# Values of two pairs of heads in one product of 512 columns, two blocks of tokens per period; a ring of seven weight tiles, three buffers of values

## The reference, cut to what matters

```python
x = x + attn(cond(x, fside, fside, w, u, cond_512))
x = x + ffn(cond2(x, ...))          # silu(x W1') * (x W3'), fwht, W2'

def attn(y):                        # y as (2, 1024, 512): 16 heads of 128
    q, k, v = y @ Wq, y @ Wk, y @ Wv            # each to 16 heads x 128
    for seg in 8 segments of 128 tokens:        # mem, z carried on
        att_dot = softmax(causal(q k' / sqrt(128))) @ v
        att_mem = (elu(q)+1) @ mem / ((elu(q)+1) @ z)
        delta   = v - (elu(k)+1) @ mem / ((elu(k)+1) @ z)
        mem, z  = mem + (elu(k)+1)' @ delta, z + sum(elu(k)+1)
        out     = (beta * att_mem + (1-beta) * att_dot) @ Wo
```

## Time and profile before

| | before |
|---|---|
| median of 3 runs | 1582.96 us (1582.52 to 1583.41) |
| profiled execution | span 1581.4 us; its own time is that span and 1.6 us around it, 1583.0 us |
| PE busy | 1547.0 us (98%), 9574 matmuls |
| DVE, ACT, POOL busy | 77%, 49%, 39% |
| a period without Wo | about 26.3 us |
| a burst period | about 48.7 us |
| period 0 starts, period 31 starts | 60.1 us, 1038.7 us |

### The profile page before, as it was taken

One profiled execution on the slowest core, in us unless ns is written; L12 is line 12 of the kernel. 1 busy time (PEld: TensorE's weight loads), 2 busy tenths in 40 slices (PEclk: granted clock), 3 DMA queues, 4 the chain that ended last, 5 costly groups with the idle time before them and its releaser, 6 DMA issues.

```text
span 1581.4 us, 26868 instructions
## 1 busy us (share of the span) xinstructions
PE 1547.0 (98%) x9574; PEld 1377.9 (87%) x9574; DVE 1219.7 (77%) x2719; ACT 782.1 (49%) x1687; POOL 615.2 (39%) x433
## 2 busy tenths in 40 slices
PE   4899999999999999999999999999999999999999
PEld 2699989999999999998999999989888888888887
DVE  8889888787878888778775773665897888687785
ACT  3576566445535626535546552653554443344442
POOL 3666585322222222222001000134664465666662
PEclk9999999999999999999999999999999999999999
DMA  5375685595473485474467547348211222311111
GB/s 177 124 246 191 223 292 195 180 392 184 161 276 127 154 286 201 147 254 160 174 228 280 210 171 283 110 141 279 88 54 54 60 89 72 107 46 62 54 41 54
DMA packets 109381, 262.04 MB, mean 166 GB/s; under 512 B 11200, under 2 KB 36160, under 8 KB 107840
## 3 DMA queue, kind: packets, MB, share of 16 engines
q1 hardware_dynamic: 90384, 227.28, 40.5%
q10 hardware_dynamic: 18864, 33.04, 6.5%
HBM read 212.03 MB, written 48.25 MB: 165 GB/s over the span
## 4 chain that ended last, share of the span: by engine, by line
PE 90%; DVE 6%; issue 2%; DMA 1%; ACT 1%; POOL 0%; SPq 0%; ACTq 0%; DVEq 0%
PE psG L595 17%; PE psG L597 17%; PE psG L596 17%; PE psX L771 4%; PE psX L726 3%; PE psX L595 3%; PE psX L597 3%; PE psX L596 3%; PE psZ L752 3%; PE psZ L743 3%; PE psZ L751 2%; PE psZ L597 2%; PE psY L597 2%; PE psY L596 2%; PE psZ L596 2%
## 5 line engine op out<-in xcount | busy, mean ns | idle before, releaser
L2076 POOL TENSOR_TENSOR wl<-stage,wh 128x512 fp32r<-128x512 f32 x160 | 233.5, 1481 | 147.4 <-ACT wh L1597 144.7
L595 PE MATMUL psG<-yh,wh 128*128 128x512 f32 x646 | 263.1, 407 | 0.0
L597 PE MATMUL psG<-yh,wl 128*128 128x512 f32 x646 | 253.0, 392 | 0.0
L596 PE MATMUL psG<-yl,wh 128*128 128x512 f32 x646 | 252.1, 390 | 0.0
L2144 POOL TENSOR_TENSOR vs<-v,omb 128x512 f32<-128x512 f32 x64 | 92.1, 1460 | 388.9 <-PE psX L726 216.0
L597 PEld LDWEIGHTS psG<-yh,wl 128*128 128x128 f32 x646 | 121.3, 188 | 26.8
L595 PE MATMUL psG<-wh,yh 128*128 128x256 f32 x480 | 141.6, 295 | 0.0
L595 PEld LDWEIGHTS psG<-yh,wh 128*128 128x128 f32 x646 | 121.9, 189 | 20.9 <-DVE sg L1274 0.3
L596 PEld LDWEIGHTS psG<-yl,wh 128*128 128x128 f32 x646 | 121.9, 189 | 20.5
L597 PE MATMUL psG<-wh,yl 128*128 128x256 f32 x480 | 135.7, 283 | 0.0
L596 PE MATMUL psG<-wl,yh 128*128 128x256 f32 x480 | 135.7, 283 | 0.0
(11 more groups left out here) (279 smaller groups left out, 4291.6 us busy)
## 6 DMA issues: line engine op xcount, KB each, us to landing
wh<-high_o SPq DMA_DIRECT2D x52, 512.0 KB, 3.6
wl<-low_o SPq DMA_DIRECT2D x52, 512.0 KB, 4.7
stage<-in_w SPq DMA_DIRECT2D x64, 256.0 KB, 3.1
wh<-high_k SPq DMA_DIRECT2D x23, 512.0 KB, 3.7
wl<-low_k SPq DMA_DIRECT2D x23, 512.0 KB, 5.0
wh<-high_q SPq DMA_DIRECT2D x23, 512.0 KB, 4.1
wl<-low_q SPq DMA_DIRECT2D x23, 512.0 KB, 5.8
wh<-high_v SPq DMA_DIRECT2D x22, 512.0 KB, 4.0
```

Source lines behind the costliest of these rows:

```text
L595: e.matmul(out, lh, rh, start=first, stop=False, skip_group_check=check)
L596: e.matmul(out, lh, rl, start=False, stop=False, skip_group_check=check)
L597: return e.matmul(out, ll, rh, start=False, stop=last, skip_group_check=check)
L2076: e.tensor_tensor(lo, raw, hi, ALU.subtract).then_inc(p_wl, 1)
```

## The change

- **Values.** `v_block` takes the place of `v_part`: one call makes values of two pairs of heads (`couple(n)` and the next) for 128 tokens. The moving operand has 512 columns: 256 from each of two tiles of the ring, through one view of the array `parts` (`parts[:, p, x:y+1:y-x, ...]`). Periods 2m and 2m+1 each make two of the four blocks of 128 tokens (`tokens_of`). The calls of a part of 12 matmuls of 256 columns become parts of 6 of 512. Periods 0 and 30 are `bare`: period 0 makes its values at its end, period 30 makes none.
- **Ring.** `wh` and `wl` become one array `parts` with 7 tiles (`NRING`). A tile of values is held over two periods (`held`), except after a burst, where the second period fetches it again as kind "w". The stream grows from 204 to 218 tiles.
- **Buffers.** The two buffers of values become one array of six halves; `HALVES` says which two a period reads.
- **Order of the stream.** k, q before v in period 0; v, v, (o...), k, q in even periods; k, q in odd ones (w, w first after a burst); k, v, v, q in period 6 (`SWAPPED`), where values also stand behind the keys on PE. The places up to which ACT, POOL and SP go follow from `ENDS`.
- **Others.** The scan tiles (1, 0, 1..3) come after (0, 2, 0..3); some semaphores are merged; `dynamic_dma_scratch_size=1024`.

```diff
-NRING = 6
+NRING = 7
...
+def couple(n):
+    return n + 2 - n % 2
+def tokens_of(n, half):
+    return 2 * (n % 2) + half
+def value_kind(n):
+    return "w" if n % 2 and is_burst(n - 1) else "v"
 def weight_stream():
...
+        a = couple(n)
+        values = [(value_kind(n), a), (value_kind(n), a + 1)]
+        has = a < NN and (n % 2 == 0 or is_burst(n - 1))
+        keys = [("k", n + 1), ("q", n + 1)]
+        if n == 0:
+            stream += keys + values
+        elif n == SWAPPED:
+            stream += keys[:1] + values + keys[1:]
+        else:
+            if has:
+                stream += values
+            if is_burst(n):
+                stream += [("o", 8 * (n // 4 - 1) + i) for i in range(8)]
+            stream += keys
...
-            def v_part(n, half, part):
-                b, i = n // NG, PLACE["v", n]
+            def v_block(n, half, part):
+                i, k = value_tiles(n)
                 if part == 0:
                     wait_split(w, i)
-                    wait_y(b)
-                    w.wait_ge(a_qm, 2 * (n - 1) + half + 1)
-                rows = slice(256 * half + 128 * part, 256 * half + 128 * part + 128)
-                for c in range(NC):
-                    cols = slice(256 * c, 256 * c + 256)
-                    m = three(G[half][:, 256 * part:256 * part + 256], yh[b % 2][:, c, rows], yl[b % 2][:, c, rows],
-                              hi[:, cols], lo[:, cols], c == 0, c == NC - 1)
+                    wait_split(w, k)
+                    wait_y(couple(n) // NG)
...
+                rows = slice(128 * tokens_of(n, half), 128 * tokens_of(n, half) + 128)
+                x, y = SLOT[i], SLOT[k]
+                for c in (0, 1) if part == 0 else (2, 3):
+                    hi, lo = (parts[:, p, x:y + 1:y - x, 256 * c:256 * c + 256] for p in range(2))
+                    m = three(G[half][:, :], yh[b % 2][:, c, rows], yl[b % 2][:, c, rows], hi, lo, c == 0, c == NC - 1)
...
-                split_hi(here + 3)
+                split_hi(o + 2 if burst else end - 1 if more else end)     # ACT, between exp_s(n, 0) and exp_s(n, 1)
...
-                keep(here + 2)
-                load_w(here + (6 if burst and n > 4 else 4))
+                keep(o + 1 if burst else end - 2)
+                load_w((o + 5 if n > 4 else o + 3) if burst else end + 1)
```

More of the change, by code:

```diff
@@ L189, with value_tiles, value_halves, blocks_by @@
 SLOT, BEFORE = places()
+def value_tiles(n):
+    return sorted((PLACE[value_kind(n), couple(n) + p] for p in range(2)), key=SLOT.__getitem__)
+def value_halves():
+    at = {0: (0, 1), 1: (2, 3)}
+    for a in range(2, NN, 2):
+        one = sorted(at[a - 3] if a > 2 else (4, 5))
+        two = sorted(at[a - 2])
+        at[a], at[a + 1] = (one[0], two[0]), (one[1], two[1])
+    return at
+HALVES = value_halves()
+def blocks_by(n, half):
+    return 2 * n + half + 1
+def values_of(n):
+    return 0 if n < 2 else blocks_by(n // 2 * 2 - 1, 1)
+def pick(t, x, y):
+    return t[:, x:y + 1:y - x] if x < y else t[:, x:y - 1 if y else None:y - x]
 def first_of(kind, m):
@@ L269, in adaln_attn_ffn @@
         yl = [sb(ctx, f"yl{i}", [P, NC, T], F32R) for i in range(2)]
[L270 to L271 removed]
+        parts = sb(ctx, "parts", [P, 2, NRING, 1024], F32R)
         stage = [sb(ctx, f"stage{i}", [P, 512]) for i in range(NSTAGE)]
@@ L321, in adaln_attn_ffn @@
         sk = sb(one, "sk", [P, 2, T])
-        v = [sb(one, f"v{i}", [P, NSEG, 2, VW]) for i in range(2)]
+        v = sb(one, "v", [P, 6, 2, 2, VW])
         vs = sb(one, "vs", [P, NSEG, 2, P])
@@ L898, in tensor @@
                     kq_part(nx, "q", 1, 1)
+                if n == 0:
+                    for half in range(2):
+                        v_block(n, half, 0)
+                        v_block(n, half, 1)
             w.wait_ge(v_f1, 2)
@@ L1913, in scalar @@
                 if burst:
-                    copy_v(nx, 1)
-                split_hi(here + 4)
+                    copy_v(n, 1)
+                split_hi(o + 3 if burst else end if more else end + 1)
                 behind(n, 3)
-                if more and n > 0 and not burst:
-                    copy_v(nx, 1)
+                if n == SWAPPED:
+                    copy_kq(nx, "k", 1, G[1])
+                    exp_kq(nx, "k", 1, G[1])
+                elif more and not bare and not burst:
+                    copy_v(n, 1)
                 if burst:
-                    split_hi(here + 6)
+                    split_hi(o + 5)
                 copy_pt(n)
@@ L1946, in scalar @@
                 if more:
-                    split_hi(here + (12 if burst else 6))
+                    split_hi(end + (1 if burst else 2))
                     copy_kq(nx, "q", 0, G[0])
                     exp_kq(nx, "q", 0, G[0])
-                    split_hi(here + (14 if burst else 6))
+                    split_hi(end + (3 if burst else 2))
                     copy_kq(nx, "q", 1, G[1])
+                    if n == 0:
+                        exp_kq(nx, "q", 1, G[1])
                 else:
@@ L2190, in gpsimd @@
                 more = nx < NN
-                here = PLACE["v", nx] if more else PLACE["1", 0]
+                end, o = ENDS[n], ENDS[n] - 10
                 if n >= LATE_V:
@@ L2194, in gpsimd @@
                 behind(n, 0)
-                split_w(here + 3)
+                split_w(o + 2 if burst else end - 1 if more else end)
                 behind(n, 1)
@@ L2200, in gpsimd @@
                     euv(4)
-                split_w(here + 4)
+                split_w(o + 3 if burst else end if more else end + 1)
                 behind(n, 3)
                 if burst:
-                    split_w(here + 6)
+                    split_w(o + 5)
                 behind(n, 4)
-                split_w(here + (9 if burst else 5))
+                split_w(o + 8 if burst else end + 1 if more else end + 2)
                 behind(n, 5)
@@ L2210, in gpsimd @@
                 if burst:
-                    split_w(here + 11)
+                    split_w(end)
                 if n == 4:
@@ L2215, in gpsimd @@
                 if burst:
-                    split_w(here + 13)
+                    split_w(end + 2)
                 if more:
-                    split_w(here + (14 if burst else 6))
+                    split_w(end + (3 if burst else 2))
                 else:
```

234 lines of the change are left out of this document (142 added, 92 removed).

## The result

The changed kernel takes 1610.73 us (median of 5 runs, 1607.71 to 1613.79) against 1582.96: a ratio of 1.0175, interval [1.0164, 1.0187]. It is slower by 27.8 us; 13.8 were forecast, and 1605 was the end of the range. The direction and four of the five periods with new waits were right; two sizes were not, and one wait was not in the sum. The profiled execution spans 1608.4 us, 27.0 more than before.

What follows compares the result with a forecast made beforehand. PE was taken as the bound, busy 1547.0 of 1581.4 us. Terms -6.0 + 9.0 + 1.5 + 4 + 3 + 2.3 = +13.8 on 1583.0 gave 1596.8, said as 1597; range 1584 to 1605.

Steps and rivals of the forecast that it cites:

- A: Matmuls of values in 30 periods: 120 parts, each 0.05 us shorter with 512 columns, 6.0 us less.
- the small gap cost: Rival: a matmul's own cost is small, wide values matmuls save some 2 us in all, 1601 us; chance 0.05.
- the two pieces: Rival: a moving operand in two pieces costs 65 us over 720 matmuls, 1648 us; chance 0.02.
- B: Period 0: later load of values 2, split between ACT's exponentials, makes PE wait for the second one: +9.0 us.
- C: Behind period 0's wait: PE's matmuls run at the lower clock for a while, +1.5 us.
- D: Period 4: the copy of P on ACT stands behind one more split tile, 19 instead of 18, +4 us.
- the signs: What would show it: PE's waits in periods 0, 4 (on pT or a Wo tile) and 6, low clock, shorter period 30.
- E: Period 6: values wait for y's low part, behind POOL's split of queries 7, +3 us.
- F: Period 30: values no longer fill between the memory's steps, so PE waits, +2.3 us.
- the fifth: Rival: waits in periods 4 and 6 pass on to the o tiles behind them, above 1606 us; chance 0.05.

Runs made afterwards that it cites:

- wide_alone: Kernel before, only the values' matmuls reshaped to 6 of 512 columns per part, orders and ring kept, values not the reference's: 1578.23 us, ratio 0.9969.
- experiment 1: Changed kernel with period 0's old order: values 2 loaded before queries 1 are kept, and split behind both exponentials: 1600.31 us.
- experiments 2 and 3: Changed kernel with one half of period 0's old order each, only the earlier load of values 2, or only its later split: 1604.47 and 1607.0 us.
- experiment 5: Changed kernel with tile o0 split on ACT and POOL at the end of period 3 instead of between period 4's exponentials: 1606.55 us.
- Experiment 6: Changed kernel with ACT's split of keys 6 moved behind the copy of the last queries, into period 5: 1607.35 us.
- y_first: Changed kernel with POOL's split of queries 7 in period 6 put behind the low part of y: 1606.22 us.
- p0_split_only: Changed kernel with values 2 split behind both exponentials of period 0, but still loaded only after keeping queries 1: 1607.0 us.
- q_copy_first: The same run as Experiment 6: changed kernel, last queries copied ahead of the split of keys 6: 1607.35 us.
- four_orders: Changed kernel with four order edits together: period 0's old order, y first in period 6, o0 split early, last queries copied first: 1587.20 us.
- y_slack: Changed kernel with all order edits: four_orders plus moved period 30 keys, scan steps, POOL's scaling, period 6 values and period 4 EUV: 1581.06 us.
- p0_order: The same run as experiment 1: changed kernel with period 0's old load and split order: 1600.31 us.

## Why the prediction was wrong

- **A (-6.0)** was right in kind and near in size. In the table 4.7 us are read in periods 1 to 3 and 7 to 29, and some 0.6 more stand within periods 4 to 6; wide_alone, where nothing else changes, gives 4.9 (3.0 to 6.8). Of the rivals the small gap cost and the two pieces are out.
- **B and C (+9.0, +1.5)** were right in place and mechanism: the wait grew by 9.8. Period 0 without 5.9 us for its values grew by 11.2; experiment 1 takes out 12.0, of which 2.2 are more than the wait, so C's 1.5 was a little low. That load and place are both needed was argued from one row; experiments 2 and 3 show that each leaves a wait of its own, on the next split. (The fixed cost that stands behind B from the Trainium skill, DMA: Bandwidth & Descriptors, section Anatomy of one DMA, is given there for DMAs that GpSimd issues; these loads are issued by SyncE, and the sum did not use it.)
- **D (+4)** measured 5.9, and its working does not hold. The count is wrong: up to o4 the stream has 17 tiles before the change, not 18, and 19 after it, so the copy of P stands behind two tiles more. By the working's own 4.7 us a tile that would be 8.5. Nor does that pace set the lateness. The tiles lay landed in their stage buffers until their place on ACT came: values 6 from about 151 to 169.21 and values 7 from about 159 to 175.16 (the rows below), o0 from 176 to 185.67, some 9 us, and the next load went out only behind such a split (o0's at 171.36). I had this order and did not price it. PE met the lateness at Wo's tiles, which the signs had named beside P. Only o0's place was tested (experiment 5); that of values 6 and 7 was not.
- **Period 5 (+4.0)** had no term. With E it is the step that failed most: "where a split stands ahead of something that PE needs" was asked of period 0 only. The same question at the end of period 4 gives keys 6 ahead of the copy of qT. Experiment 6 takes out all of it.
- **E (+3)** measured 8.0. The working gave 4.3 to 5.2 us of wait; I then cut it to 3 for short waits that it would replace, with no row for them, and charged no clock. Measured: 6.5 of wait, for POOL's rows were longer (5.6 for 4.2), and about 2 of clock, as y_first shows.
- **F (+2.3)** came out: 2.1 us of waits in two rows, period 30 shorter by 3.5. There was luck in it: with the same waits the period takes 1.5 us more in half of the traces (last section).

```profile
169.21 1.14 ACT L1695 ACTIVATE parts<-stage 128x512 fp32r<-128x512 f32 x2
...
175.16 1.14 ACT L1695 ACTIVATE parts<-stage 128x512 fp32r<-128x512 f32 x2
```

Together: D 1.9, period 5 4.0, E 5.0, B and C 0.7, the start 0.7, and A 1.3 short in its rows less 0.5 that the end gave make 13.1 of the 13.2 us between +13.8 and the span's +27.0. The rival that came nearest was the fifth, at a chance of 0.05. Its way (D passed on) was not the true one: separate places were.

## What to carry to other kernels

When the order of a stream of tiles changes, go through each engine's queue and list every instruction that waits for a load or a split and has something of the critical engine's behind it; price all of them, with the lower clock behind each wait that is longer than those already in the trace. Look also at how long a landed tile lies until its place comes. A small gain on a saturated engine (5 us here) needs every such place right: the same wide matmuls gave 4.9 us with the old order, lost 27.8 with the new one, and won 2.0 with its places mended. Don't net an estimated wait against others without a row for them.

## What was not expected of the hardware

Waits cost more than their length, and not the same each time. The same wait of 1.32 us in period 30, in the changed kernel and in y_first:

```profile
1050.61 0.47 PE L872 MATMUL psX<-HH,had 128*128 128x512 f32 x1 [1.32 <-DVE HL L1231]
```

```profile
1043.97 0.77 PE L872 MATMUL psX<-HH,had 128*128 128x512 f32 x1 [1.32 <-DVE HL L1231]
```

Behind the second the matmuls run at the lower clock for a while, and the period takes 26.60 us instead of 25.07. Its window in y_first (columns as in the earlier trace rows; the changed kernel's, at 1.00, stands above):

```profile
1035.10:1061.70 26.60, 24.47 (x145) 21.12 (x144) 15.48 (x54) 17.85 (x44) 8.07 (x6) 0.94 0.16 51
```

Eight traces have these same waits in period 30 (0.8 and 1.3 us). In four of them the period takes 25.1 us at a clock of 1.00, in four (y_first, p0_split_only, q_copy_first, four_orders) 26.5 to 26.7 at 0.94. Period 4 shows the same: 54.6 us at 1.00, and 56.4 at 0.97 in y_first with the same waits.

The changed kernel's five executions spread over 6.1 us. With the waits mended, y_slack's eleven spread over 2.3, like the kernel before measured beside it (2.2 in sixteen). That the spread comes from such draws is likely: p0_order's fastest execution, 1594.73, had a mean granted clock of 0.997, its slowest two, 1602.3, had 0.993. No run tests it alone.
